# A Mamba block with expert weights: both ends of the schedule reordered, two decays of each group made five units ahead

## The chip, the cores and the metric

The kernel runs on one core of a Trainium2 chip. The metric is the device time of one execution in microseconds (us). Before the change it is 1063.78 us, the median of three runs (1063.17 to 1065.88).

## The reference, cut to what matters

For 32 sequences of 128 tokens and 128 channels, all in float32: rotate pairs of channels, normalise, run a selective scan forwards and backwards (16 states for each of 256 inner channels), mix both, gate, add the input; then an expert layer whose weights are picked by the sequence, and a feed-forward net of five layers.

```python
def _mamba(x, ...):
    xz = x @ in_proj_w.T;  xi, z = (xz[..., :DI], xz[..., DI:])
    xi = silu(causal_conv(xi, conv_w) + conv_b)
    dt, Bm, Cm = split(xi @ x_proj_w.T)
    delta = softplus(dt @ dt_proj_w.T + dt_proj_b);  A = -exp(A_log)
    # for each state n: h = exp(delta*A[n])*h + delta*xi*Bm[n];  y += h*Cm[n]
    y = (selective_scan(xi, delta, A, Bm, Cm) + xi * D) * silu(z)
    return y @ out_proj_w.T
y = gelu(concat(_mamba(xn), flip(_mamba(flip(xn)))) @ dim_reduce_w.T + b)
g = y @ glu_w.T + glu_b;  y = g[..., :H] * sigmoid(g[..., H:]) + skip
h = relu(x @ wi_e.T) @ wo_e.T                      # weights of expert e
h = silu(h @ w1.T * s1) * (h @ w2.T * s2)
h = gelu(h @ h1.T * s);  h = gelu(h @ h2.T * s);  out = x + h @ w3.T * s
```

## The kernel before

The sequences go through in nine groups: one of 2 sequences (256 columns), seven of 4 (512 columns), and one of 2 again. A group has 32 units: 16 states forwards (d = 0), 16 backwards (d = 1). Unit u passes through the engines in this order:

- GpSimd writes the drive of the unit, `du * b_row`, to one of 8 state rooms in SBUF (`drive`, L555), up to three units ahead.
- ScalarE writes the decay `exp(a_n * delta)` to one of two PSUM rooms `bank_d[u % 2]` in two instructions (`decays`, L702), two units ahead (`DECAY_LEAD`); before it the room must be free, so it waits for the product of unit u-2.
- VectorE scans (`scan`): for most units in place in the PSUM room (L905), then it multiplies by the row of C into the state room (L910). For the seven units of `POOL_UNITS` (3, 8, 12, 17, 21, 26, 30) the scan writes to the state room (L903), and GpSimd multiplies by the row of C (`weigh`, L560).
- TensorE adds the products up by transposes in PSUM (`sum_states`, L1190). After 16 units ScalarE copies the sum, and TensorE turns it back and adds `u * D` by a matmul with a diagonal matrix (`turn_y`, L1199 and L1201); VectorE multiplies by the gate (`gate_y`, L921).
- The rows of B and C come by DMA from DRAM, broadcast to all partitions, each kind into a ring of six rows.

All other layers are "fills": one PSUM bank filled by TensorE and taken by ScalarE or VectorE. Two banks (`bank_m`) serve all fills in turn. The order is written out by hand: every engine walks the same timeline in steps of half a unit, and the tables `FILL`, `TAKE_LAG`, `ACT_AT`, `VEC`, `GPS` and `LOADS` say at which time, counted in units from the start of its group, an engine issues each piece; `FIRST_GROUP`, `NEXT_TO_LAST` and `LAST_GROUP` shift it for groups 0, 7 and 8. The later layers of a group therefore run during the scans of the next two groups: the second Gelu layer of group g (`h2_`, taken by L751, Gelu at L758) is issued at 63 to 71, that is in the units 31 to 39 behind its own start of scans, while group g+1 ends and group g+2 begins. The tables set only the order on each engine; the times follow from semaphores.

ScalarE's functions come in table sets. Decays need the exponential set, the silu and the gelu another each, and each change is an `ACT_TABLE_LOAD` (L586).

For the ends: in group 0 both directions' inputs, the gates z and both halves are filled before the first scan; `step_sizes` (L535) and `inputs` (L544) on GpSimd make `delta` and `du` for both directions. In group 7 the h2 fills stand at 34 to 35 of group 8, ahead of the last `turn_y` at 36. The sigmoid of every group is made from exponential, logarithm and exponential (L719, L726, L728).

## Time and profile before

| what | value |
|---|---|
| median of three runs | 1063.78 us |
| the profiled execution: its own time | 1062.9 us |
| the profiled execution: span | 1060.6 us |
| mean granted TensorE clock | 0.96 of full speed |
| busy: TensorE, VectorE, ScalarE, GpSimd | 89%, 86%, 73%, 78% |
| chain that ended last | TensorE 46%, VectorE 19%, ScalarE 17%, issue 15%, GpSimd 3% |
| first scan, end of the last product of VectorE | 34.65 us, 1001.55 us |
| table loads of ScalarE | 69, 88.5 us |

The span runs from the first to the last instruction; the execution's own time is 2.3 us longer. The busy shares are means over three different stretches: a head without scans, the scans, and a tail in which only the late layers of groups 7 and 8 are left. The chain runs over all engines in turn, so a single share says little.

### The profile page before, as it was taken

Reading aid. Unit: us, or ns where it says so; the run is one execution under the profiler, and the core shown is the slowest. Engines: PE = TensorE matmul, PEld = TensorE weight load, DVE = VectorE, ACT = ScalarE, POOL = GpSimd, SP = SyncE. Lnnn points to the kernel's source line nnn. Section 1 sums busy time; section 2 is a strip of 40 time slices with the busy share of each in tenths; the row PEclk is TensorE's granted clock in tenths of the full one; section 3 lists DMA queues with packets and bytes.
Section 4 is the critical chain, followed back from the end, with each engine's and each line's share of the span. In section 5 each row is a group of like instructions: output and inputs, shape, how many; then the busy total and the mean of one; then the engine's idle time right before and its main releaser. Section 6 shows DMA issues by size and latency. Waiting matters only on the chain.

```text
span 1060.6 us, 13662 instructions
## 1 busy us (share of the span) xinstructions
PE 943.8 (89%) x4312; PEld 599.0 (56%) x4312; DVE 908.4 (86%) x718; ACT 778.1 (73%) x1233; POOL 829.5 (78%) x430
## 2 busy tenths in 40 slices
PE   5698678778999899999999999999999988998987
PEld 3455455656655467445755566545755575556455
DVE  1788999999999989999999999998999999968600
ACT  4757667778698768877688868877788758777532
POOL 0767998989988897989878997979878998866300
PEclk9697699898999999999999999999999999999999
DMA  3766675463646555654556554745555465536000
GB/s 95 253 204 208 187 216 180 137 218 116 195 142 194 171 165 147 208 167 144 160 163 183 168 167 123 237 147 168 153 164 187 151 178 146 165 121 169 0 11 6
DMA packets 97670, 167.43 MB, mean 158 GB/s; under 512 B 9920, under 2 KB 33408, under 8 KB 97344
## 3 DMA queue, kind: packets, MB, share of 16 engines
q1 hardware_dynamic: 97600, 166.57, 50.8%
q8 instruction: 35, 0.57, 0.2%
q14 instruction: 35, 0.29, 0.1%
HBM read 159.19 MB, written 7.34 MB: 157 GB/s over the span
## 4 chain that ended last, share of the span: by engine, by line
PE 46%; DVE 19%; ACT 17%; issue 15%; POOL 3%; DMA 0%; DVEq 0%; SPq 0%; POOLq 0%; ACTq 0%
DVE bank_d L905 12%; PE bank_m L1102 9%; PE bank_m L1026 9%; PE bank_y L1190 8%; ACT L586 5%; ACT bank_d L702 5%; PE bank_m L1109 5%; PE bank_m L1116 2%; DVE state L903 2%; PE bank_m L1075 2%; PE bank_m L1084 2%; DVE state L910 2%; POOL state L555 2%; PE bank_m L1044 1%; PE bank_m L1059 1%
## 5 line engine op out<-in xcount | busy, mean ns | idle before, releaser
L555 POOL TENSOR_TENSOR state<-du,b_rows 128x1024 f32<-128x1024 f32 (+1 forms) x288 | 603.9, 2121 | 92.6 <-PE bank_y L1190 91.7
L905 DVE TENSOR_TENSOR_SCAN bank_d<-bank_d,state 128x1024 f32<-128x1024 f32 (+1 forms) x225 | 461.2, 2050 | 44.0 <-ACT bank_d L702 38.6
L702 ACT ACTIVATE bank_d<-delta,a_neg 128x512 f32<-128x512 f32 (+1 forms) x576 | 345.0, 634 | 104.5 <-DVE state L910 94.2
L1190 PEld LDWEIGHTS bank_y<-ident,state 128*128 128x128 f32 x2048 | 240.4, 145 | 81.7 <-issue 55.5
L1190 PE MATMUL bank_y<-ident,state 128*128 128x128 f32 x2048 | 263.3, 281 | 17.8 <-POOL state L560 11.7
L910 DVE TENSOR_TENSOR state<-bank_d,c_rows 128x1024 f32<-128x1024 f32 (+1 forms) x225 | 248.8, 1106 | 7.8
L560 POOL TENSOR_TENSOR state<-state,c_rows 128x1024 f32<-128x1024 f32 (+1 forms) x63 | 134.2, 2131 | 16.4 <-DVE state L903 16.4
L903 DVE TENSOR_TENSOR_SCAN state<-bank_d,state 128x1024 f32<-128x1024 f32 (+1 forms) x63 | 128.7, 2042 | 1.2 <-ACT bank_d L702 1.2
L1109 PE MATMUL bank_m<-hidA,h_s 128*128 128x512 f32 (+1 forms) x256 | 111.8, 584 | 15.6 <-ACT relu_dt L683 9.7
L1026 PE MATMUL bank_m<-xnT,w_conv 128*128 128x508 f32 (+7 forms) x288 | 115.3, 550 | 4.8 <-DVE x1T L930 3.1
L1102 PE MATMUL bank_m<-hidB,h_s 128*128 128x512 f32 (+1 forms) x256 | 110.3, 584 | 1.7 <-DVE hidB L944 0.8
L586 ACT ACT_TABLE_LOAD x69 | 88.5, 1283 | 1.9 <-PEq L1266 0.7
L1109 PEld LDWEIGHTS bank_m<-hidA,h_s 128*128 128x128 f32 x256 | 48.3, 197 | 69.3 <-issue 50.7
L1026 PEld LDWEIGHTS bank_m<-xnT,w_conv 128*128 128x128 f32 x288 | 54.1, 195 | 51.0 <-issue 43.1
L1102 PEld LDWEIGHTS bank_m<-hidB,h_s 128*128 128x128 f32 x256 | 48.5, 194 | 56.0 <-issue 52.3
L535 POOL TENSOR_TENSOR delta<-relu_dt,log_dt 128x1024 f32<-128x1024 f32 (+1 forms) x18 | 38.2, 2122 | 24.5 <-ACT log_dt L693 24.5
L1044 PE MATMUL bank_m<-dbc,w_dt_s 64*128 64x512 f32 (+1 forms) x72 | 37.5, 612 | 15.0 <-ACT dbc L677 12.6
L751 ACT ACTIVATE hidB<-bank_m,col 128x512 f32<-128x512 f32 (+1 forms) x32 | 21.1, 661 | 34.6 <-PE bank_m L1109 34.0
L921 DVE TENSOR_TENSOR gated<-bank_y,z 128x1024 f32<-128x1024 f32 (+1 forms) x18 | 19.8, 1102 | 26.5 <-PE bank_y L1201 26.5
L520 POOL TENSOR_TENSOR rstd<-var_eps,half_power 128x4 f32<-128x4 f32 (+1 forms) x9 | 8.6, 951 | 35.1 <-issue 20.1
L1075 PE MATMUL bank_m<-x1T,wsel 128*128 128x128 f32 x240 | 31.7, 278 | 3.9 <-DVE x1T L934 3.5
L1075 PEld LDWEIGHTS bank_m<-x1T,wsel 128*128 128x128 f32 x240 | 29.6, 191 | 7.7 <-DVE x1T L930 3.9
(143 smaller groups left out, 1011.8 us busy)
## 6 DMA issues: line engine op xcount, KB each, us to landing
b_rows<-bc_store SPq DMA_DIRECT2D x256, 256.0 KB, 4.2
c_rows<-bc_store SPq DMA_DIRECT2D x256, 256.0 KB, 4.3
wsel<-merged SPq DMA_DIRECT2D x32, 512.0 KB, 3.5
merged<-hidA SPq DMA_DIRECT2D x8, 512.0 KB, 3.1
h_s<-in_h SPq DMA_DIRECT2D x2, 1024.0 KB, 8.9
xin<-in_x SPq DMA_DIRECT2D x7, 256.0 KB, 3.9
out<-cT SPq DMA_DIRECT2D x7, 256.0 KB, 3.1
wsel<-in_factors SPq DMA_DIRECT2D x8, 160.0 KB, 3.7
```

What stands on the lines that cost most here:

```text
L555: nc.gpsimd.tensor_tensor(split(unit_state(u)), du[:, d, :, :width(g)], per_half(b_rows, u), ALU.mult).then_inc(S.bx_ready, 1)
L560: nc.gpsimd.tensor_tensor(split(unit_state(u)), split(unit_state(u)), per_half(c_rows, u), ALU.mult).then_inc(S.weighed, 1)
L586: act.preload_act_table_set(name)
L702: ins = act.activation(split(unit_decay(u))[:, h], delta[:, d, h, :width(g)], ACT.Exp, scale=a_neg[:, h, n:n + 1])
L903: dve.tensor_tensor_scan(drive, decay, drive, 0.0, ALU.mult, ALU.add).then_inc(S.unit_done, 1)
L905: dve.tensor_tensor_scan(decay, decay, drive, 0.0, ALU.mult, ALU.add).then_inc(S.scanned, 1)
L910: dve.tensor_tensor(split(unit_state(u)), split(unit_decay(u)), per_half(c_rows, u), ALU.mult).then_inc(S.unit_done, 1)
L1026: ins = pe.matmul(dst, w, src, start=(m == 0), stop=(m == TAPS - 1))
L1075: ins = pe.matmul(bank(g, f"hid{f}")[:, at], wsel[:, s, f * P:(f + 1) * P], x1T[:, at], start=True, stop=True)
L1102: ins = pe.matmul(bank(g, f"h1_{f}"), h1_s[:, q, f * P:(f + 1) * P], hidB[:, q, :width(g)], start=(q == 0), stop=(q == FC - 1))
L1109: ins = pe.matmul(bank(g, f"h2_{f}"), h2_s[:, q, f * P:(f + 1) * P], hidA[:, q, :width(g)], start=(q == 0), stop=(q == FC - 1))
L1190: ins = pe.matmul(bank_y[:, h, s * P:(s + 1) * P], split(unit_state(u))[:, h, s * LEN:(s + 1) * LEN], ident[:, :], start=(n == 0 and s == ...
```

## The change

- `early`, a room in SBUF of 1024 columns: the decays of units 8 and 17 of every group (`AHEAD`) are made there five units ahead instead of two. The other units share the two PSUM rooms in turn, so the first units behind 8 and 17 wait for one unit earlier than before. The ring of C rows falls from six to four to make room.
- `u * D` of groups 7 and 8 goes through ScalarE (`skip`): a scaled copy into `gated`, added up by transposes with the states; the matmul with the diagonal goes.
- Group 0: VectorE makes `delta` and `du` of d = 0 (`first_inputs`); `ur` and `z` are filled behind the inputs of d = 0, `ur` gets its Silu in a second step (`front` at 4.0). The conv weights are made behind `rotate`.
- Group 7's second Gelu layer is taken with Gelu from the bank; its fills h2_0 to h2_3, w3 and tok move to 75, 68, 78.5, 81.5, 82.5 and 88, that is into the chain of group 8's late layers (h2_1 at 36.0 of group 8, behind the turn, then out at 36.5, glu1 37.5, glu0 39, h2_0 43, res 44, hid 44.5 to 46, h2_2 46.5, wo 48, h2_3 49.5).
- Group 8's sigmoid is half of tanh plus a half, with the gelu's table set.
- Slots move by half a unit or so in the inner groups, by more in groups 0, 1 (a new table `SECOND_GROUP`), 7 and 8. In the inner groups `out` is issued at 37.5 instead of 38.0 and the second Gelu at 70.5 instead of 71.0.

```diff
-ROWS = 6
+ROWS, C_ROWS = 6, 4
+AHEAD, AHEAD_LEAD = (8, 17), 5
-DIRECT = {"gate": NG - 1, "h1_": NG - 1, "h2_": NG - 1}
+BY_SCALAR = NG - 2
+DIRECT = {"gate": NG - 1, "h1_": NG - 1, "h2_": NG - 2}
...
+        early = sb("early", [P, HALVES * GT])
...
+        def ahead(u):
+            return u % UNITS in AHEAD
+        in_psum = [u for u in range(TOTAL) if not ahead(u)]
+        psum_at = {u: i for i, u in enumerate(in_psum)}
+        in_early = [u for u in range(TOTAL) if ahead(u)]
...
         def unit_decay(u):
-            return bank_d[u % 2][:, :HALVES * width(u // UNITS)]
+            room = early if ahead(u) else bank_d[psum_at[u] % 2]
+            return room[:, :HALVES * width(u // UNITS)]
...
                 use_table(EXP_LN)
-                if n == 0:
+                if n == 0 or ahead(u):
                     act.wait_ge(S.starts_marked, 2 * g + d + 1)
-                wait(act, S.unit_done, u - 1)
+                before = [v for v in in_early if v < u][-1:] if ahead(u) else in_psum[:psum_at[u]][-2:-1]
+                if before:
+                    act.wait_ge(S.unit_done, before[0] + 1)
...
+            def skip(g, d):
+                wait_u(act, g, d)
+                if g > 0:
+                    wait_filled(act, g - 1, "out")
+                w = width(g)
+                for h in range(HALVES):
+                    ins = act.activation(gated[:, d, h, :w], (u_f, u_r)[d][:, g % 2, h, :w], ACT.Copy, scale=c("skip_d", h))
+                ins.then_inc(S.skipped, 1)
...
+            def first_inputs():
+                w = width(0)
+                dve.wait_ge(S.log_ready, 1)
+                dve.tensor_tensor(delta[:, 0, :, :w], relu_dt[:, :, :w], log_dt[:, :, :w], ALU.add).then_inc(S.delta_ready, 1)
+                dve.wait_ge(S.delta_ready, 1)
+                wait_u(dve, 0, 0)
+                dve.tensor_tensor(du[:, 0, :, :w], delta[:, 0, :, :w], u_f[:, 0, :, :w], ALU.mult).then_inc(S.du_ready, 1)
...
+                if n == NST - 1 and g >= BY_SCALAR:
+                    pe.wait_ge(S.skipped, 2 * (g - BY_SCALAR) + d + 1)
+                    for h in range(HALVES):
+                        for s in range(sequences(g)):
+                            pe.matmul(bank_y[:, h, s * P:(s + 1) * P], gated[:, d, h, s * LEN:(s + 1) * LEN], ident[:, :],
+                                      start=False, stop=False, is_transpose=True, skip_group_check=True)
...
+            dve.wait_ge(S.exp_done, made_as[u] + 1)
```

## Rows read from the trace of the kernel before

**Rows 1.** The page's first part: busy time and share of each engine.
```profile
PE 943.8 (89%) x4312; PEld 599.0 (56%) x4312; DVE 908.4 (86%) x718; ACT 778.1 (73%) x1233; POOL 829.5 (78%) x430
```

**Rows 2.** Busy time by stretch (us, PE, PEld, DVE, ACT, POOL, PEclk, DMA, GB/s).
```profile
0.00:34.60 34.60, 18.16 (x64) 13.30 (x64) 6.01 (x25) 18.45 (x44) 6.11 (x14) 0.97 0.40 120
...
262.00:379.00 117.00, 108.90 (x504) 66.06 (x503) 111.69 (x78) 94.62 (x141) 103.35 (x48) 1.00 0.55 173
...
1001.60:1018.20 16.60, 15.93 (x44) 7.63 (x44) 0.00 (x0) 4.90 (x7) 0.00 (x0) 1.00 0.00 0
1018.20:1061.00 42.80, 33.25 (x149) 24.36 (x148) 4.57 (x9) 15.59 (x27) 0.00 (x0) 0.99 0.04 10
```

**Rows 3.** Groups of VectorE's instructions by shape: GpSimd-weighed units, full width.
```profile
L903 DVE TENSOR_TENSOR_SCAN state<-bank_d,state 128x1024 f32<-128x1024 f32 x49 | 111.7, 2279 | 0.6 <-ACT bank_d L702 0.6
```

**Rows 4.** Waits of VectorE, 262 to 846 us (total, times, longest).
```profile
DVE bank_d L905 <- ACT bank_d L702: 21.8, 12, 2.2
DVE x1T L930 <- PE bank_m L1059: 3.5, 4, 0.9
DVE gated L921 <- PE bank_y L1201: 3.2, 6, 0.6
```

**Rows 5.** VectorE's timeline: scans of units 8 and 9, group 5.
```profile
605.19 2.28 DVE L903 TENSOR_TENSOR_SCAN state<-bank_d,state 128x1024 f32<-128x1024 f32 x1
609.59 2.30 DVE L905 TENSOR_TENSOR_SCAN bank_d<-bank_d,state 128x1024 f32<-128x1024 f32 x1 [2.13 <-ACT bank_d L702]
```

**Rows 6.** The timeline of ScalarE between the decays of units 8 and 9.
```profile
601.84 1.30 ACT L702 ACTIVATE bank_d<-delta,a_neg 128x512 f32<-128x512 f32 x2 [0.44 <-DVE state L910]
...
603.16 1.28 ACT L586 ACT_TABLE_LOAD   x1
...
604.46 1.91 ACT L758 ACTIVATE hidB<-hidB 128x2048 f32<-128x2048 f32 x1
...
608.26 1.30 ACT L702 ACTIVATE bank_d<-delta,a_neg 128x512 f32<-128x512 f32 x2
```

**Rows 7.** VectorE instructions with both inputs in SBUF, and GpSimd beside them (timeline).
```profile
114.20 1.40 DVE L883 TENSOR_TENSOR xc<-xc,scaled 128x512 f32<-128x512 f32 x1
...
343.38 0.68 DVE L883 TENSOR_TENSOR xc<-xc,scaled 128x512 f32<-128x512 f32 x1
...
110.40 4.66 POOL L555 TENSOR_TENSOR state<-du,b_rows 128x1024 f32<-128x1024 f32 x2
115.01 1.72 POOL L560 TENSOR_TENSOR state<-state,c_rows 128x512 f32<-128x512 f32 x1
```

**Rows 8.** GpSimd beside the scans of units 8 and 17, group 5 (timeline).
```profile
602.73 7.00 POOL L555 TENSOR_TENSOR state<-du,b_rows 128x1024 f32<-128x1024 f32 x3
...
640.99 2.36 POOL L555 TENSOR_TENSOR state<-du,b_rows 128x1024 f32<-128x1024 f32 x1 [1.91 <-PE bank_y L1190]
...
639.24 2.28 DVE L903 TENSOR_TENSOR_SCAN state<-bank_d,state 128x1024 f32<-128x1024 f32 x1
```

**Rows 9.** The page's DMA issues: KB each, median us from issue to landing.
```profile
c_rows<-bc_store SPq DMA_DIRECT2D x256, 256.0 KB, 4.3
```

**Rows 10.** The timeline of the head, to the first scan.
```profile
13.17 2.05 PE L1032 MATMUL bank_m<-xnT,w_z_s 128*128 128x256 f32 x4 [0.75 <-ACT xnT L634]
...
15.01 9.04 PE L1026 MATMUL bank_m<-xnT,w_conv 128*128 128x256 f32 x32
...
30.52 1.26 POOL L535 TENSOR_TENSOR delta<-relu_dt,log_dt 128x512 f32<-128x512 f32 x1 [19.63 <-ACT log_dt L693]
...
34.65 1.23 DVE L905 TENSOR_TENSOR_SCAN bank_d<-bank_d,state 128x512 f32<-128x512 f32 x1 [4.64 <-POOL state L555]
```

**Rows 11.** Waits of VectorE, 925 to 1001.6 us.
```profile
DVE bank_d L905 <- ACT bank_d L702: 10.7, 6, 4.0
```

**Rows 12.** TensorE's timeline behind the last scan.
```profile
1002.93 13.97 PE L1109 MATMUL bank_m<-hidA,h_s 128*128 128x512 f32 x32 [0.67 <-ACT hidA L758]
...
1016.74 0.59 PE L1199 MATMUL bank_y<-u_r,skip 128*128 128x256 f32 x2
```

More of the change, by code:

```diff
@@ L133, in slot @@
     at = table[name] if k is None else table[name][k]
-    shifts = {0: FIRST_GROUP, NG - 2: NEXT_TO_LAST, NG - 1: LAST_GROUP}.get(g, {})
-    return at + shifts.get(name, 0.0)
+    shifts = {0: FIRST_GROUP, 1: SECOND_GROUP, NG - 2: NEXT_TO_LAST, NG - 1: LAST_GROUP}.get(g, {})
+    return at + shifts.get(name, 0.0) + (0.0 if k is None else shifts.get(f"{name}:{k}", 0.0))
 def first_pair(g):
@@ L280, in wait_u @@
         def wait_u(eng, g, d):
-            if g == 0:
-                wait_taken(eng, g, *(("uf0", "uf1"), ("ur0", "ur1"))[d])
+            if g + d == 0:
+                wait_taken(eng, g, "uf0", "uf1")
             else:
-                eng.wait_ge(S.u_ready, 2 * (g - 1) + d + 1)
+                eng.wait_ge(S.u_ready, 2 * g + d)
         def wait_hidden(eng, g, name):
@@ L531, in step_sizes @@
             def step_sizes(g, d):
+                if g + d == 0:
+                    return
                 wait(pool, S.log_ready, 2 * g + d + 1)
-                wait(pool, S.exp_done, UNITS * (g - 1) + NST * d + NST)
+                if g > 0:
+                    pool.wait_ge(S.exp_done, max(made_as[UNITS * (g - 1) + NST * d + n] for n in range(NST)) + 1)
                 w = width(g)
@@ L764, in table_of @@
             def table_of(g, name):
-                if g == 0 and name[0] == "u":
+                if g == 0 and name[:2] == "uf":
                     return SILU
                 if name == "glu1":
-                    return EXP_LN
+                    return EXP_LN if g < NG - 1 else GELU
                 if name == "out" or name[:3] in ("h1_", "h2_") and direct(g, name[:3]):
@@ L822, in _ @@
                     for d in range(2):
+                        if g >= BY_SCALAR and rel == slot(ACT_AT, g, "skip", d):
+                            skip(g, d)
                         if rel == slot(ACT_AT, g, "softplus", d):
@@ L827, in _ @@
                 for g, rel in groups[::-1]:
-                    if rel == slot(ACT_AT, g, "silu", 0):
+                    if rel == slot(ACT_AT, g, "front"):
                         silu_front(g)
-                    if not direct(g, "gate") and rel == slot(ACT_AT, g, "silu", 1):
+                    if not direct(g, "gate") and rel == slot(ACT_AT, g, "silu"):
                         silu_gate(g)
                 for g, rel in groups[::-1]:
-                    if rel == slot(ACT_AT, g, "silu", 0):
+                    if rel == slot(ACT_AT, g, "front"):
                         silu_z(g)
                 u = unit_at(at, DECAY_LEAD)
-                if u is not None:
+                if u is not None and not ahead(u):
+                    decays(u)
+                u = unit_at(at, AHEAD_LEAD)
+                if u is not None and ahead(u):
                     decays(u)
@@ L969, in _ @@
             rotation_tables()
-            conv_weights()
-            skip_weights()
             for at, groups in timeline():
+                if at == slot(GPS, 0, "delta", 0):
+                    first_inputs()
                 u = unit_at(at, 0)
```

95 lines of the change are left out of this document (53 added, 42 removed), and 47 rows, old and new, of tables (FILL, FIRST_GROUP, LAST_GROUP, NEXT_TO_LAST).

## The prediction
> **What bounds the kernel now.** The page's busy shares [rows 1] name TensorE, but the busy time by stretch splits the span into three parts with different limits [rows 2]. In the head (34.6 us) no engine is busy for more than 18.5 us: it is a chain of dependent steps up to the first scan. From 34.6 to 1001.6 us VectorE is the bound: in an inner group it is busy 111.7 of 117 us, TensorE 108.9, GpSimd 103.4, ScalarE 94.6. In the tail TensorE is the bound: 15.93 + 33.25 = 49.2 us busy of 59.4. So a gain can come from a shorter chain ahead of the first scan, from VectorE's waits in between, or from TensorE's work and gaps behind the last scan; and the inner groups can give little, since TensorE would be the bound at 109.
>
> Then the waits of VectorE over the five inner periods, 262 to 846 us [rows 4]: 21.8 us in 12 waits for ScalarE's decays, 3.5 and 3.2 us for two TensorE results. That is 5.7 us per group. The timeline says which decays are late: five of the twelve stand ahead of unit 9 and take 2.12 us each [rows 5], the rest stand ahead of unit 0 (1.6 to 2.2 us) and unit 27. ScalarE's own timeline shows why unit 9 is late [rows 6]: the decay of unit 8 waits for the product of unit 6 (begins at 601.84), then come the table load, the Gelu of 2048 columns, another take and another table load, and the decay of unit 9 begins only at 608.26.
>
> **Decays made ahead: the gain.** With unit 8's decay made at unit 3, the table load can follow unit 7's decay. From 603.16 it moves up by the 1.30 us of unit 8's decay and the wait of 0.44 ahead of it, 1.7 us; `out` is issued one unit earlier, so the take behind the Gelu should not hold this up. Unit 9's decay would then end near 607.9 and its scan could begin at 608.0 instead of 609.6: about 1.5 of the 2.12 us. The waits ahead of units 0 and 27 come from the first Gelu at 29.5, whose place in the order is as before; I leave them. Unit 17 has no wait of this kind in any inner group, so its early decay gains nothing there. Bound from below: all waits ahead of unit 9 gone, 1.0 (group 2) + 5 x 2.12 + 4.0 (group 8, the longest of [rows 11]) = 15.6 us.
>
> **Decays made ahead: the cost.** The early room is in SBUF, and the drive is in SBUF too, so the scans of units 8 and 17 read two SBUF operands; before, every scan read its decay from PSUM. The only VectorE instruction of the inner loop with both inputs in SBUF is L883 [rows 7]. Where GpSimd is idle it takes 0.68 us. At 114.20 it took 1.40 us: GpSimd's instruction ran until 115.06, and VectorE ended 0.54 us after that; GpSimd's next instruction, 1.26 us long elsewhere, took 1.72 us and began its real work when VectorE was through. The two shut each other out for whole instructions. So an early scan waits for what is left of GpSimd's instruction (0 to 2.3 us), and then holds GpSimd up for its own 2.28 us [rows 3].
>
> What is left can be read at the same places of this trace. For unit 8 of group 5, GpSimd is in the second of three drives of 2.33 us each, which ends 2.2 us behind the scan's start; for unit 17 GpSimd waits for TensorE and nothing is left [rows 8]. Read in the same way in all nine groups: unit 8: 0.7, 0.8, 1.2, 2.1, 2.1, 2.2, 2.1, 0, 0.9; unit 17: 0.75, 1.5, 0, 0, 0, 0, 0, 2.1, 0.5. Now the sum. In groups 3 to 6 a scan 8 that starts 2.1 us late ends at 609.6, exactly when scan 9 began before: gain and cost cancel, 0. Group 2: +0.2. Groups 0 and 1, where nothing waited at unit 9: +1.5. Group 7: nothing left, -1.5. Group 8: 4.0 of wait, 0.9 of cost, and part of the ScalarE chain stays: -2.5. Unit 17 in all: +4.9. Together +2.6 us. The bounds: -15.6 us (no exclusion and every wait gone), and with the full 2.3 us at 14 full-width scans and 1.25 us at four narrow ones, 37 us, less the 10 us of waits they fall on, +27 us. I take +2.6, which rests on the phases of this very trace, though the phases will move.
>
> The Trainium skill has this rule in "SBUF — State Buffer", section "Who interferes with whom": a VectorE instruction with two SBUF inputs contends with a GpSimd instruction that reads SBUF, and whichever is first holds the shared pair until its instruction ends. By that rule the cost stands as summed here; without it group 2 would give 1.0, the inner groups 5 x 1.5 and group 8 about 3 us, which makes the total 14 us lower. The row at 114.20 agrees with the rule.
>
> GpSimd loses up to 2 x 2.28 us per group. It is busy 103.4 of 117, and its drives are waiting for TensorE to free state rooms, so 4.6 of 13.6 us of slack go. Near unit 9 the drives are two units ahead (about 7 us): no new wait of VectorE.
>
> **Four rows of C.** The load for unit u now waits for the product of u-4 instead of u-6; the queue of SP holds the loads of B behind it. A load lands in 4.3 us at the median [rows 9], three units last over 10 us, and for a unit weighed by GpSimd still two units are left: 0, at most 2 us per group if GpSimd falls behind.
>
> **The head.** Removed ahead of the first scan: the z fills (2.05 us) and half of the 9.04 us of conv fills, 4.5 us [rows 10]; `rotate` starts 0.9 us earlier, since it no longer stands behind the conv weights; `delta` and `du` on VectorE take 0.68 us each by [rows 7] instead of 1.26 us each [rows 10], -1.2 us. That is -8.6 us for the drive. But on ScalarE the takes of ur0, ur1, z0 and z1 stand ahead of the first decay, and on VectorE two merges of expert weights stand ahead of the first scan, the second ready only near 29.1 us. So I get the first scan at 29.8 instead of 34.65: -4.85 us, and one merge (0.65) that used to interrupt the scans is already done: -5.5 us. Group 0 itself pays: two more table loads (2 x 1.28 [rows 6]) and a Silu at slot 4.0, of which two units of lead hide most, and GpSimd's delta of d = 1 has to wait for a softplus later in ScalarE's order: +1 (-3 to +5).
>
> **The end of the scans.** VectorE waits 10.7 us for decays in group 8 [rows 11]; one of the six is counted above. Group 8's slots are mostly new; the diagonal matmuls go (0.59 us a piece at this width [rows 12], double that in group 7) and the transposes that replace them cost about half. ScalarE has eight more copies. I take -2.5 us (-7 to +4).
>
> **The tail.** The last turn waits for 13.97 us of h2 fills of group 7 [rows 12]. That is no gain of 14 us: the fills are only moved behind it, and TensorE's 49.2 us must all be done. What can go is the 10.2 us of gaps: the last 2.7 are the final copy and store, the three between the deep layers of group 8 (0.6 each) have no filler, and the ones around out, hid, wo and gate, near 3 us, get h2 fills. Two diagonal matmuls (1.2 us) go, 0.4 us of transposes come. -2.5 - 0.8 = -3.3 us (-1 to -7). The tanh form saves two table loads that lay beside 3.6 us of TensorE work: 0.
>
> **The sum.** +2.6 - 5.5 + 1 - 2.5 - 3.3 = -7.7 us against the profiled execution: a span of 1052.9 and an own time of 1055.2 us. Its 1062.9 stands 0.9 us below the median, so on the runs' scale I say 1056.
>
> **Rivals.**
> (A) The exclusion hardly hurts: early scans start just ahead of GpSimd's instructions instead of just behind (it is 0.13 to 0.26 us in groups 3 to 6), and then GpSimd waits, not VectorE. Ahead-decays give -8 instead of +2.6, less the 10.3 us of the ends, total -18: 1045. For it: small phase shifts decide it. Against: GpSimd is busy 88% in these groups.
> (B) The exclusion decides: each early scan waits 1.5 us or more and GpSimd's lost 4.6 us per group make its products late, so that TensorE, busy 93% and in order, sums late and everything behind slips. Place: units 8 to 12 and 17 to 20 of each full group. 14 x 2 us = +28 - 10 = +18, less 10.3 at the ends: +8, 1071. It decides from a mean wait of about 1.4 us per early scan. Against: unit 17 finds GpSimd idle in five groups.
> (C) The ends are worth nothing: group 0 gives back what the head gained (d = 1 late), and the reordered group 8 waits elsewhere. Then only +2.6 - 3.3: 1063, no change.
>
> **Chances.** Forecast 0.45, A 0.20, B 0.18, C 0.17. My forecast's own range is 1050 to 1062. 0.3%, about 3.2 us, is what a measurement here can tell from no change. Faster: most of the forecast (0.43), all of A, a little of C: 0.65. Same: 0.14. Slower: B and a part of C: 0.21. The range, 1043 to 1070, takes in A and nearly all of B.
>
> **What would show it.** First scan near 30 us. Scans that read `early` longer than 2.28 us, up to 4.6, beside a running GpSimd instruction, and GpSimd's instructions beside them up to 2.3 us longer; period of an inner group 116 to 117. The last gate within 5 us of the last product, with h2 fills between the layers of group 8, and 55 to 57 us from the last product to the end. I am wrong if early scans all take 2.28 us, if the period leaves 115 to 118, or if the scans of group 0 begin earlier and end no earlier.

## The result, and the profile after

The changed kernel takes 1060.55 us (median of six runs, 1059.2 to 1064.38) against 1063.47 for the kernel before in the same job (1062.82 to 1065.88): a ratio of 0.9969, 95% interval 0.9958 to 0.998. It is faster by 2.9 us where 7.7 were forecast. The stated range held the time; the sum behind it did not stand. The profiled execution has a span of 1057.0 us, 3.6 less than before.

The page's first part, after (as [rows 1]):

```profile
PE 944.2 (89%) x4320; PEld 603.2 (57%) x4320; DVE 920.4 (87%) x722; ACT 779.4 (74%) x1241; POOL 855.6 (81%) x428
```

VectorE and GpSimd are busy 12.0 and 26.1 us longer, though each does about the same work. This is how it looks when one engine is shut out while its instruction already counts as running. The groups of VectorE's scans say where (columns as in [rows 3]):

```profile
L978 DVE TENSOR_TENSOR_SCAN state<-bank_d,state 128x1024 f32<-128x1024 f32 x35 | 79.8, 2280 | 1.5 <-ACT bank_d L745 1.5
L978 DVE TENSOR_TENSOR_SCAN state<-early,state 128x1024 f32<-128x1024 f32 x14 | 41.3, 2953 | 0.0
```

The same line takes 2280 ns with the decay in PSUM and 2953 ns with the decay in SBUF. At full width that is 14 x 0.67 = 9.4 us; the four narrow ones (256 columns) add 2.0.

An inner period by stretch (columns as [rows 2]): TensorE and ScalarE do no more than before, VectorE 1.5 and GpSimd 4.0 us more.

```profile
262.00:379.00 117.00, 108.69 (x504) 65.97 (x504) 113.14 (x78) 92.52 (x138) 107.30 (x48) 1.00 0.56 167
```

The waits of VectorE over the same five periods as [rows 4], in this kernel 254 to 836.5 us:

```profile
DVE bank_d L980 <- ACT bank_d L745: 13.2, 9, 1.9
DVE gated L996 <- PE bank_y L1286: 5.0, 5, 2.3
DVE x1T L1026 <- PE bank_m L1194: 2.3, 1, 2.3
```

The wait for decays fell from 21.8 to 13.2 us: the 2.12 us ahead of unit 9 are gone in all these groups but group 6, where 0.88 is left. In group 5, the place of [rows 5], [rows 6] and [rows 8], the timelines of VectorE, ScalarE and GpSimd now read:

```profile
596.94 2.54 DVE L978 TENSOR_TENSOR_SCAN state<-early,state 128x1024 f32<-128x1024 f32 x1
599.40 2.27 DVE L980 TENSOR_TENSOR_SCAN bank_d<-bank_d,state 128x1024 f32<-128x1024 f32 x1
...
592.21 1.28 ACT L626 ACT_TABLE_LOAD   x1
593.50 1.92 ACT L817 ACTIVATE hidB<-hidB 128x2048 f32<-128x2048 f32 x1
595.33 0.66 ACT L765 ACTIVATE gy<-bank_m,col 128x512 f32<-128x512 f32 x1
...
592.63 9.00 POOL L595 TENSOR_TENSOR state<-du,b_rows 128x1024 f32<-128x1024 f32 x3
```

The early scan lost only 0.25 us: it began 4.31 us into GpSimd's three drives, just before the second ended. The three drives took 9.00 us instead of 7.00, so here GpSimd paid. The forecast had the scan just behind the start of the second drive and 2.2 us late.

The starts of the first scans of the groups give the periods (us, group 0 to 7): before 76.1, 112.6, 116.5, 116.8, 118.5, 117.1, 118.5, 114.0; after 76.6, 112.5, 117.3, 114.1, 115.6, 116.4, 124.0, 115.8. The first scan begins at 31.06 (before 34.65), the last at 998.7 (999.6). So 3.6 us are gained in the head and 6.3 in groups 3 to 5; 1.2 are lost in groups 0 to 2, 5.5 in group 6, 1.8 in group 7 and 0.5 in group 8's scans. In group 6 TensorE waits 3.06 us for `gy` and VectorE 2.29 for w3, and the scan of unit 17 is 1.93 us late. The tail follows, TensorE's timeline behind the last product (which ends at 1000.64; [rows 12] are before's):

```profile
1002.97 3.60 PE L1187 MATMUL bank_m<-hidA,h_s 128*128 128x512 f32 x8
1006.40 1.89 PE L1129 MATMUL bank_m<-gated,w_fused 128*128 128x256 f32 x8
1008.95 1.10 PE L1137 MATMUL bank_m<-xnT,w_glu_s 128*128 128x256 f32 x4 [0.66 <-ACT xnT L765]
1010.18 3.70 PE L1187 MATMUL bank_m<-hidA,h_s 128*128 128x512 f32 x8
...
1043.53 7.14 PE L1187 MATMUL bank_m<-relu_dt,h_s 128*128 128x256 f32 x32 [0.61 <-issue]
```

The h2 fills of group 7 stand between the layers of group 8, and 56.4 us pass from the last product to the end, where it was 59.05.

### The profile page after: what moved, and what is told of

The parts are those of the page before. It is cut to its first block, busy times and chain, and to the rows that moved or that the text cites. A ratio compares the mean times of both kernels' runs of the same rounds, so it can differ in the third digit from the quotient of the medians.

```text
span 1057.0 us, 13719 instructions
## 1 busy us (share of the span) xinstructions
PE 944.2 (89%) x4320; PEld 603.2 (57%) x4320; DVE 920.4 (87%) x722; ACT 779.4 (74%) x1241; POOL 855.6 (81%) x428
## 4 chain that ended last, share of the span: by engine, by line
PE 44%; ACT 17%; issue 16%; DVE 14%; POOL 8%; DMA 1%; SPq 0%; DVEq 0%; POOLq 0%; ACTq 0%
DVE bank_d L980 9%; PE bank_y L1274 9%; PE bank_m L1104 8%; PE bank_m L1180 7%; POOL state L595 5%; PE bank_m L1187 5%; ACT bank_d L745 4%; ACT L626 4%; PE bank_m L1153 3%; DVE state L978 2%; POOL state L600 2%; PE bank_m L1194 2%; PE bank_m L1162 2%; PE bank_m L1169 2%; PE bank_m L1122 1%
## 5 line engine op out<-in xcount | busy, mean ns | idle before, releaser
L595 POOL TENSOR_TENSOR state<-du,b_rows 128x1024 f32<-128x1024 f32 (+1 forms) x288 | 629.1, 2210 | 53.6 <-PE bank_y L1274 46.1
L980 DVE TENSOR_TENSOR_SCAN bank_d<-bank_d,state 128x1024 f32<-128x1024 f32 (+1 forms) x225 | 461.2, 2050 | 32.0 <-ACT bank_d L745 30.9
L745 ACT ACTIVATE bank_d<-delta,a_neg 128x512 f32<-128x512 f32 (+1 forms) x540 | 322.6, 634 | 78.2 <-DVE state L985 73.5
L1274 PEld LDWEIGHTS bank_y<-ident,state 128*128 128x128 f32 x2048 | 243.9, 147 | 92.5 <-issue 63.4
L1274 PE MATMUL bank_y<-ident,state 128*128 128x128 f32 x2048 | 270.2, 284 | 25.9 <-DVE gated L996 12.5
L600 POOL TENSOR_TENSOR state<-state,c_rows 128x1024 f32<-128x1024 f32 (+1 forms) x63 | 134.1, 2128 | 16.7 <-DVE state L978 15.7
L1104 PE MATMUL bank_m<-xnT,w_conv 128*128 128x508 f32 (+7 forms) x288 | 118.4, 557 | 4.5 <-DVE x1T L1005 2.4
L1187 PE MATMUL bank_m<-hidA,h_s 128*128 128x512 f32 (+1 forms) x256 | 112.5, 585 | 5.7 <-ACT hidA L817 4.6
L1180 PE MATMUL bank_m<-hidB,h_s 128*128 128x512 f32 (+1 forms) x256 | 107.8, 573 | 0.8 <-DVE hidB L1019 0.8
L978 DVE TENSOR_TENSOR_SCAN state<-bank_d,state 128x1024 f32<-128x1024 f32 (+1 forms) x45 | 92.0, 2044 | 3.4 <-ACT bank_d L745 3.4
L576 POOL TENSOR_TENSOR delta<-relu_dt,log_dt 128x1024 f32<-128x1024 f32 (+1 forms) x17 | 38.9, 2287 | 13.1 <-ACT log_dt L733 13.1
L978 DVE TENSOR_TENSOR_SCAN state<-early,state 128x1024 f32<-128x1024 f32 (+1 forms) x18 | 48.2, 2678 | 0.0
L1169 PE MATMUL bank_m<-cT,w_s 128*128 128x512 f32 (+1 forms) x64 | 32.1, 625 | 10.1 <-ACT hidA L801 9.6
```

The source lines that it names most:

```text
L595: nc.gpsimd.tensor_tensor(split(unit_state(u)), du[:, d, :, :width(g)], per_half(b_rows, u), ALU.mult).then_inc(S.bx_ready, 1)
L600: nc.gpsimd.tensor_tensor(split(unit_state(u)), split(unit_state(u)), per_half(c_rows, u), ALU.mult).then_inc(S.weighed, 1)
L745: ins = act.activation(split(unit_decay(u))[:, h], delta[:, d, h, :width(g)], ACT.Exp, scale=a_neg[:, h, n:n + 1])
L978: dve.tensor_tensor_scan(drive, decay, drive, 0.0, ALU.mult, ALU.add).then_inc(S.unit_done, 1)
L980: dve.tensor_tensor_scan(decay, decay, drive, 0.0, ALU.mult, ALU.add).then_inc(S.scanned, 1)
L1104: ins = pe.matmul(dst, w, src, start=(m == 0), stop=(m == TAPS - 1))
```

## The experiments

All were timed against the kernel before in the same job and on the same chip, each 4 to 12 times (before's medians there: 1064.2 to 1065.1). "Ends" is everything in the change but the early decays and the C ring, so it includes the half-unit moves of the inner groups. Differences below are differences of ratios times 1064 us.

| kernel | median, us | ratio to before, 95% |
|---|---|---|
| E1 ends, no early decay, C ring 4 | 1077.99 | 1.0117 [1.0101, 1.0133] |
| E2 before + early 8 and 17, C ring 4 | 1078.89 | 1.0138 [1.0116, 1.0159] |
| E3 before, 8 and 17 in SBUF but two ahead, C ring 4 | 1078.14 | 1.0118 [1.0095, 1.0141] |
| E4 after, early 8 alone | 1054.51 | 0.9896 [0.9882, 0.9911] |
| E5 before + C ring 4 | 1068.04 | 1.0030 [1.0018, 1.0042] |
| E6 ends, no early decay, C ring 6 | 1076.24 | 1.0103 [1.0084, 1.0122] |
| E7 E4 with rings of 5 and 5 | 1054.94 | 0.9908 [0.9883, 0.9934] |
| E8 after, early 8 and 30 | 1059.82 | 0.9961 [0.9945, 0.9977] |
| E9 E6 with before's slots in groups 2 to 6 | 1075.09 | 1.0107 [1.0091, 1.0123] |
| E10 before + early 8 alone, C ring 4 | 1066.85 | 1.0013 [1.0000, 1.0026] |
| E11 E4 with before's slots in groups 2 to 6 | 1064.31 | 1.0000 [0.9987, 1.0013] |
| E12 E4 with group 7's late fills ahead of the turn | 1061.76 | 0.9967 [0.9955, 0.9980] |
| E13 ends, 8 in SBUF but two ahead | 1074.39 | 1.0080 [1.0058, 1.0103] |
| E14 after, early 17 alone | 1081.03 | 1.0154 [1.0129, 1.0180] |
| E15 E4 with the decay three units ahead | 1058.54 | 0.9939 [0.9917, 0.9961] |
| E16 E4 with the conv weights ahead of `rotate` | 1055.21 | 0.9909 [0.9883, 0.9934] |

### The change taken apart

E1 is the new kernel with no unit made early, E2 the old one with the early decays added, E3 the old one with nothing but the room changed:

```diff
# E1
-AHEAD, AHEAD_LEAD = (8, 17), 5
+AHEAD, AHEAD_LEAD = (), 5
# E3, in before (with C_ROWS = 4)
-            return bank_d[u % 2][:, :HALVES * width(u // UNITS)]
+            room = early if u % UNITS in (8, 17) else bank_d[u % 2]
+            return room[:, :HALVES * width(u // UNITS)]
```

> The changed kernel without decays made ahead: all decays in the two PSUM rooms, two units ahead; the reordered ends and the four rows of C stay. Theory 1 (the exclusion of VectorE and GpSimd takes back what the early decays gain): this kernel is as fast as the changed one, 1060.5 us, within 2 us, and the period of groups 3 to 5 is back at 116.8 us, but no scan takes over 2.31 us. Theory 2 (the early decays gain 8 us or more and the reordered ends cost it): this kernel is slower than the changed one by 5 us or more, at 1065 or above. The first scan stays at 31.1 us by both.

> The kernel before, with only the decays of units 8 and 17 made five units ahead in SBUF and four rows of C; every slot, head and tail as before. Theory 1: about 1063 us (within 2 us of before): waits ahead of unit 9 fall by 1.5 to 2 us in groups 2 to 8, scans of units 8 and 17 take up to 4.6 us. Theory 2: 1056 us or less. First scan at 34.65 us by both.

> The kernel before, the decays of units 8 and 17 written to the SBUF room, but two units ahead and with the waits of before: the price of the exclusion without any gain; four rows of C. By the phases read in the trace of before (16.8 us of remains, of which 4 x 2.1 us at unit 8 fall ahead of a wait for the decay of unit 9, which they do not shorten): +13 to +17 us, 1077 to 1080, if the wait for unit 9 follows the scan of unit 8; if the decay of unit 9 is ready meanwhile (it does not wait for unit 8), the late scan 8 uses up that wait, and only +5 to +8 us stay, 1069 to 1071. If there is no exclusion: 1063.5, no change. Scans of 8 and 17 between 2.28 and 4.6 us, and GpSimd's instructions beside them up to 4.6 us.

E1 is 1.17% slower than before, not 10 us faster, so the ends alone cost, and the early decays give back 1.48% (15.7 us) on top of them. E2 shows the opposite in the old slots; at 1078.9 us it is 16 us above the slower of its two expectations. The exclusion is real: in E3 nothing moved but the room (and the C ring), and scan 8 of groups 3 to 6 takes 4.22 to 4.34 us. E3's time fell in the first of its branches, its trace in the second: the late scan used up the wait ahead of unit 9 (0.1 to 0.2 us left). All 18 early scans together are 23.5 us longer than their PSUM form in E3, 21.6 in E2 and 11.4 in the changed kernel. In E2 scan 8 is as long as in E3, and GpSimd's timeline beside it shows the phase:

```profile
607.67 8.99 POOL L567 TENSOR_TENSOR state<-du,b_rows 128x1024 f32<-128x1024 f32 x3
```

```profile
610.21 4.31 DVE L920 TENSOR_TENSOR_SCAN state<-early,state 128x1024 f32<-128x1024 f32 x1
```

This scan begins 2.54 us into the three drives, just behind the start of the second, and waits 2.03 us for it: the 2.1 us of the forecast. In the changed kernel it began 4.31 us into them and lost 0.25. GpSimd's three drives take 9.0 us in both.

The wait is not bounded by one instruction of the other engine. In group 1 of E3 and of E10 (below; unit 8 alone, old slots) scan 8 took 7.60 and 7.64 us. E10's VectorE and GpSimd there:

```profile
140.87 7.64 DVE L920 TENSOR_TENSOR_SCAN state<-early,state 128x1024 f32<-128x1024 f32 x1
...
137.05 7.00 POOL L567 TENSOR_TENSOR state<-du,b_rows 128x1024 f32<-128x1024 f32 x3
144.03 2.34 POOL L556 TENSOR_TENSOR du<-delta,u_r 128x1024 f32<-128x1024 f32 x1
```

The scan stood through the rest of the second drive, the third, and `du`, though both of the latter began behind it. In E2 a scan with the same start (140.87) took 3.00 us. No run shows what decides between the two.

### Unit 8 alone, and the ring of C rows

E4 has `AHEAD = (8,)`, E5 is the kernel before with `C_ROWS = 4`, and E6 is E1 with `C_ROWS = 6`.

> The changed kernel with only unit 8's decay made ahead; unit 17's goes back to PSUM, two units ahead. Unit 17 gained nothing at its place and cost scans of 4.49, 4.21, 4.00 and 2.82 us instead of 2.28 in groups 2, 6, 7 and 1, 6.4 us. Theory 1: faster than the changed kernel by 3 to 6 us, 1055 to 1058. Rival (the waits behind unit 17 are TensorE's and come anyway, as the turn of group 6 at 765.6): within 1.5 us of the changed kernel.

> The kernel before with four rows of C instead of six and nothing else. Theory 1 (the short ring is what made the last four kernels slow: the load of C for unit u stands in SP's queue until GpSimd has weighed unit u-4, and the loads of B behind it come late): slower than before by 8 to 14 us, 1072 to 1078, and SP's waits for the weighing of L560 rise from 119 us to about 200 in 262 to 846 us. Theory 2 (the ring costs nothing, the exclusion costs 14 us in the one kernel and the reordered ends 14 us in the other): within 2 us of before.

> The changed kernel without early decays and with six rows of C: the reordered ends alone. Theory 1: the ends bring what their places show, 3.6 us ahead of the first scan and 2.7 behind the last product, so 1056 to 1059, and the kernel with four rows (1078) was slow by its ring. Theory 2: still at 1074 or more.

E4 has the lowest median of all: 1.04% below before and 0.73% (7.8 us) below the change as made, a little more than expected. Unit 17 early only costs. E5 puts the smaller ring at +3.2 us, between its expectations. The queue of SP waits longer, 262 to 846 us, before and then E5: the load of a C row (L449, L450) now waits for the product made from the row four loads back, GpSimd's above all.

```profile
SPq L449 <- POOL state L560: 118.8, 25, 7.1
```

```profile
SPq L450 <- POOL state L561: 186.9, 27, 11.0
SPq L450 <- DVE state L911: 134.3, 64, 5.6
```

But the periods of groups 2 to 5 are before's within 0.2 us, so that is not where it costs. Groups 0, 1 and 6 are longer, by 1.6, 1.3 and 3.4 us. In group 6 what comes late is not a C row but the next x, whose load stands behind those of C in the same queue. It is issued 103.9 us into the group, just behind a C row's, instead of 98.5; ScalarE stands 4.04 us for it, and the decay of unit 29 behind it is late for VectorE:

```profile
798.92 0.32 SPq L450 DMA_DIRECT2D c_rows<-bc_store  x1
799.34 0.37 SPq L395 DMA_DIRECT2D xin<-in_x  x1
...
803.99 0.40 ACT L615 ACTIVATE scaled<-xin,rot 128x128 f32<-128x128 f32 x1 [4.04 <-DMA xin<-in_x]
...
806.49 2.30 DVE L906 TENSOR_TENSOR_SCAN bank_d<-bank_d,state 128x1024 f32<-128x1024 f32 x1 [3.92 <-ACT bank_d L703]
```

With the ends the ring's share (E1 against E6) is 0.14%, within the intervals. So E6, the ends with nothing else, costs about 11 us. Its profiled execution is 16.0 us longer than before's: head and group 0 gain 5.2, group 8 and the tail 1.8, and groups 1 to 6 lose 3.0, 5.8, 5.2, 1.9, 2.3 and 4.7.

### Where one early decay gains 23 us

E1 against E4 is one decay per group: 2.21%, 23.5 us (22.2 in the two profiled executions). The waits ahead of unit 9 account for a part: 2.1 to 2.3 us in each of groups 3 to 7, 16.9 us in all nine groups of E1 and 3.7 in E4. TensorE's timeline in group 3, E1:

```profile
377.66 1.63 PE L1137 MATMUL bank_m<-gy,w_glu_s 128*128 128x512 f32 x2 [4.06 <-ACT gy L765]
...
379.93 2.68 PE L1274 MATMUL bank_y<-ident,state 128*128 128x128 f32 x16
382.45 3.60 PE L1194 MATMUL bank_m<-hidB,w_s 128*128 128x512 f32 x8
```

and VectorE's in E1:

```profile
380.16 2.30 DVE L980 TENSOR_TENSOR_SCAN bank_d<-bank_d,state 128x1024 f32<-128x1024 f32 x1 [2.12 <-ACT bank_d L745]
...
386.09 0.75 DVE L1026 SCALAR_TENSOR_TENSOR x1T<-bank_m,col,x1T 128x512 f32<-128x512 f32 x1 [2.37 <-PE bank_m L1194]
```

The same place in E4, TensorE:

```profile
367.81 1.10 PE L1137 MATMUL bank_m<-gy,w_glu_s 128*128 128x512 f32 x2 [1.36 <-ACT gy L765]
...
369.19 1.91 PE L1274 MATMUL bank_y<-ident,state 128*128 128x128 f32 x16
```

Three things hang on that one decay here. VectorE waits 2.12 us ahead of unit 9. TensorE, in order, stands 4.06 us for `gy`, which ScalarE makes behind the Gelu. And TensorE's clock falls; the stretches of E1 (columns as in [rows 2]) are the one with the wait, the one behind it, and the next:

```profile
372.50:377.60 5.10, 1.09 (x9) 0.80 (x7) 5.07 (x3) 5.05 (x6) 5.10 (x3) 1.00 0.77 258
377.60:382.40 4.80, 4.74 (x22) 3.85 (x23) 2.68 (x2) 4.79 (x7) 4.74 (x4) 0.64 0.42 84
382.40:386.00 3.60, 3.60 (x11) 1.69 (x10) 1.28 (x2) 1.49 (x3) 3.60 (x3) 1.00 0.00 0
```

Behind 4.06 us of standing the granted clock reads 0.64, a mixture of the two levels, 1.2 and 2.4 GHz, and 16 transposes take 2.68 us instead of 1.91. Then w3's fill is late, and VectorE waits for it another 2.37 us. In E4 the wait is 1.36 us, the clock stays at 1.00, and w3 is in time. In the kernel before the wait was 2.34 us, the clock stayed at 1.00, and w3 was in time too.

The other groups agree on the clock and less on w3. In groups 3 to 7 of E1 the waits for `gy` are 3.66 to 4.25 us, and the lower level is granted behind each. In before it is granted behind none of the four of 2.23 to 2.34 us, but behind the 2.12 us of group 7 (0.66 from 841 to 846 us), so the length of one wait doesn't settle it alone. VectorE's wait for w3 shows only in groups 2, 3 and 6 of E1 (2.78, 2.37, 2.30 us) and in group 6 of E4 (2.30). Over the whole execution E4's VectorE waits 14.7 us less for decays (ahead of L980, 37.5 instead of 52.2 us), 5.1 less for w3 and about 6 less in smaller waits, and its early scans take 4.4 us back: 21 of the 22.2 us. Over 262 to 846 us TensorE's waits for `gy` in before, E1 and E4:

```profile
PE bank_m L1059 <- ACT gy L712: 11.4, 5, 2.3
```

```profile
PE bank_m L1137 <- ACT gy L765: 16.4, 4, 4.2
```

```profile
PE bank_m L1137 <- ACT gy L765: 7.3, 5, 3.1
```

E1 has four waits in this window, since its fifth (3.66 us) falls behind it. So the new slots had made a hidden wait long enough to come to the surface, and the early decay of unit 8 took it away again. Three runs ask which property of it does so. E10 is the kernel before with only unit 8 early; E13 keeps E1's order but puts unit 8's decay in SBUF; E15 makes it three units ahead (`AHEAD_LEAD = 3`).

```diff
# E13, in E1
-            room = early if ahead(u) else bank_d[psum_at[u] % 2]
+            room = early if u % UNITS == 8 else bank_d[u % 2]
```

> The kernel before with only unit 8's decay made ahead, and four rows of C; all slots of before. With units 8 and 17 ahead it took 1079. Scans 17 there cost 7.8 us more than 2.28 each, so -8: 1069 to 1072, if the cost is the scan's own lengthening; theory 2, GpSimd's lost time at unit 17 carries over to unit 8 of the next group (scan 8 took 4.25 us there, 2.52 in the changed kernel): below 1065.

> The kernel after the change, where the decay of unit 8 alone still goes to the SBUF room but is made two units ahead, at its old place in ScalarE's order; unit 17 is in PSUM. Theory (what helps is the place in ScalarE's order, ahead of the table load for Gelu): nothing of the 23.5 us between no early decay (1078.0) and unit 8 alone (1054.5) comes back, and the wait of scan 8 for GpSimd is added, 7 groups x 1 to 2 us: 1078 to 1090, with w3's take still waiting 2 us and more per group. Rival (the relief comes from unit 8 leaving the two PSUM rooms, or from the phase that a longer scan 8 gives to what follows): 1065 or less.

> Unit 8 alone ahead, but three units ahead instead of five: its decay is issued one unit earlier than before the change. Theory (it must only stand ahead of the table change; how far ahead does not matter): the Gelu chain still loses one decay, so 1054.5 as with five units, 1052 to 1057. Rival (distance matters: three ahead it stands just behind unit 7's decay wait, for a product that is late, and the table load moves up by less): between 1060 and 1070, with a wait of TensorE for gy near 3 us.

In the old slots it is worth 1.8 us (E10 against E5, whose intervals overlap): the wait ahead of unit 9 goes, and scan 8 takes 4.24 to 4.29 us in groups 3 to 6 instead of 2.28. In E13 the wait for `gy` is back, 4.10 us in group 4, and so is most of the time: 19.6 of the 23.5 us come with making the decay early. That moves it in ScalarE's order and also leaves a PSUM room free sooner for the decays behind it, which E13's rule does not. The trace of E4 says that the order does it: in groups 3 to 6 the decay of unit 9 begins 0.28 to 1.98 us behind the product of unit 7, which would have freed its room under the old rule too, with no wait of ScalarE in front of it. The room alone (E13 against E1) gave 3.9 us where I had expected nothing or a loss; the two intervals touch, the runs are of different jobs, and why stays open. Three units ahead is 4.6 us slower than five, between the two expectations: TensorE's waits for `gy` grow from 1.36 to about 1.87 us in groups 3 to 5 and from 3.06 to 4.29 in group 6. Its profiled span isn't longer (1055.7 against 1056.9), but E4's profiled execution (1059.1) is the slowest of its five, 4.6 us above their median, so E4's trace shows less than its runs gained.

### Other units

> The changed kernel with the decays of units 8 and 30 made ahead instead of 8 and 17. With unit 30's made early, unit 31's waits for unit 28 instead of 29, so the table load and the first Gelu at 29.5 come up to 3.4 us sooner and the wait of 1.6 to 2.2 us ahead of unit 0 of each group goes. Theory 1 (a long ScalarE piece between two decays is what makes VectorE wait, and one free room ahead of it cures that): -1 to -2 us per full group against the kernel with unit 8 alone (1054.5), 1044 to 1049, if scan 30 meets little of GpSimd's work. Rival (the exclusion at unit 30 takes it back, as GpSimd is in a row of drives there): 1053 to 1060.

> The kernel after the change with only unit 17 made five ahead; unit 8 back in PSUM two ahead. Theory (the gain is unit 8's alone, since only its decay stands in front of the table loads of Gelu and gy; unit 17 costs 6 us as it did between unit 8 alone and both): no early decay 1078.0 plus 0 to 6: 1078 to 1084. Rival (ScalarE is late all over in the reordered schedule, any decay out of its way helps, and 17 would relieve the takes around units 12 to 17): 1066 to 1072.

E8 makes unit 30 early beside unit 8. VectorE's waits for decays over 262 to 846 us, E4 and E8:

```profile
DVE bank_d L980 <- ACT bank_d L745: 19.4, 15, 3.5
```

```profile
DVE bank_d L980 <- ACT bank_d L745: 12.5, 13, 3.5
```

The waits fell by 6.9 us and the kernel became 6.9 us slower (its profiled span, 1056.3, is E4's within 0.6): less waiting for one engine is not less time. The scans of unit 30 say where a part went: they now take 2.95 to 4.13 us in groups 2 to 7 instead of 2.28, 8.5 us more in all nine groups. E14 completes the square of the two units: neither 1.0117, 8 alone 0.9896, 17 alone 1.0154, both 0.9969. Unit 17 costs 3.9 us by itself and 7.8 beside unit 8. Its scans take 4.49, 4.21 and 4.00 us in groups 2, 6 and 7 of the changed kernel; VectorE and GpSimd in group 6:

```profile
748.74 4.21 DVE L978 TENSOR_TENSOR_SCAN state<-early,state 128x1024 f32<-128x1024 f32 x1
...
746.13 8.98 POOL L595 TENSOR_TENSOR state<-du,b_rows 128x1024 f32<-128x1024 f32 x3 [2.80 <-PE bank_y L1274]
```

The scan begins 2.61 us into three drives, again just behind the start of the second. It is late by 1.93 us. No run splits the 7.8 us further.

### The slots

E9 and E11 give groups 2 to 6 the slots of the kernel before, without an early decay and with unit 8's; E12 puts `h2_0`, `h2_2`, `h2_3`, `w3` and `tok` of group 7 back ahead of the last turn (and `h2_1` one unit earlier); E7 shares the rows evenly.

```diff
# E12, in E4 (the entries that change, cut out of their lines)
-"h2_2": 13.5, "h2_3": 13.5, "w3": 10.0, "h2_0": 9.0, "tok": 14.0, "h2_1": 4.5
+"h2_2": 1.5, "h2_3": -1.0, "w3": -0.5, "h2_0": 0.0, "tok": 0.0, "h2_1": 3.5
```

> The reordered ends without early decays and with six rows of C (1076 with the new inner slots), but groups 2 to 6 at the slots of the kernel before. Theory 1 (the half-unit moves of the inner groups only pay with unit 8's decay early; without it TensorE waits 4.1 us for gy instead of 2.3, and VectorE 2.4 us for w3): the inner periods return to 116.8 to 118.5, 1060 to 1064. Theory 2 (the reordered groups 0, 1, 7 and 8 are what cost): 1072 or more.

> The changed kernel with unit 8 ahead (1054.5), groups 2 to 6 at the slots of before. Theory 1 (slots and early decay pay only together): 1062 or more, with scans 8 near 4.2 us. Rival (the inner slots are worth nothing, the early decay all): 1053 to 1056.

> The changed kernel with unit 8 ahead (1054.5), but group 7's h2, w3 and tok fills back at the slots of before, ahead of the last turn. By the sum (TensorE's work behind the last product is the same, only its gaps are filled): +2 to +4, 1056.5 to 1058.5. Rival: the fills ahead of the turn hold the whole of group 8's chain, +8 or more.

> The changed kernel with only unit 8 made ahead, and the same SBUF shared out as five rows of B and five of C instead of six and four. Theory 1 (the C ring's wait for the weighing is the cost): 1050 to 1053, against 1054.5 with six and four. Rival (B is as tight as C, since GpSimd drives three units ahead): 1057 or more.

E9 equals E6 in time, so the old inner slots alone don't give the 11 us back. In the profiles they do help where they stand, groups 2 to 6 being 9.8 us shorter than in E6, but group 7 behind them is 5.6 us longer and group 1 0.7. E11 against E4 is 11.1 us: with the early decay the new inner slots are what lets it gain. Part of that is the phase: scan 8 of groups 4 to 6 takes 4.24 to 4.32 us in E11 and 2.52 to 2.53 in E4, 5.3 us in all, which is the whole difference of the two profiled spans (5.0); the rest shows in the medians alone. E12 against E4 is 7.6 us: in the profiles the scans end 5.8 us earlier without the reorder (the last product at 994.8 against 1000.6 in E4 and after alike), and the tail is 62.3 us long instead of 56.4. That made the two profiled executions equal, and the runs put the reorder well ahead, by more than the 2 to 4 us expected. E7 is E4 within its interval, between its two expectations: the ring is not what limits E4.

### The head

`rotate` did start earlier, at 7.02 instead of 7.83 us, and yet the normalised input was ready no sooner. GpSimd's first power instruction in the changed kernel:

```profile
8.68 1.54 POOL L558 TENSOR_TENSOR rstd<-var_eps,half_power 128x2 f32<-128x2 f32 x1 [7.15 <-DVE var_eps L971]
```

Before, it took 0.71. VectorE's product of the conv weights, two SBUF inputs, ran beside it (8.43 to 9.65 us). E16 puts those weights back ahead of `rotate`:

```diff
             rotation_tables()
+            conv_weights()
+            skip_weights()
...
                         rotate(g)
-                        if g == 0:
-                            conv_weights()
-                            skip_weights()
```

> Unit 8 alone ahead, with the conv and skip weights made ahead of rotate on VectorE again, as in the kernel before the change. Theory (GpSimd's first power instruction took 1.54 us instead of 0.71 only because VectorE's weight instructions, both inputs in SBUF, ran beside it, which ate the 0.8 us that the earlier rotate had gained): rotate starts near 7.8 us, the power instruction takes 0.7 us again, xnT is ready at the same time as with unit 8 alone, the first scan starts within 0.3 us of its 31 us, and the time is 1054.5 within 2. Rival (the reorder does help the head): the first scan 0.8 us later or more.

```profile
10.09 0.71 POOL L558 TENSOR_TENSOR rstd<-var_eps,half_power 128x2 f32<-128x2 f32 x1 [8.56 <-DVE var_eps L971]
```

The power instruction takes 0.71 us again, the first scan begins at 30.59 (E4: 31.35), and the time is E4's. Moving these weights bought nothing. Nor is the earlier scan due to it: `rotate` now starts at 8.44 us, and the normalised input is ready 0.45 us later than in E4.

What moves the first scan between kernels of the same head is TensorE's clock. In the changed kernel the trace's first clock record, at full level, begins at 18.77 us. The conv matmuls start 0.42 us apart ahead of it and 0.21 us apart behind it, as they would at 1.2 and 2.4 GHz. (The view of stretches prints a clock of 1.00 for the time without a record.) In E1 the first record begins at 16.27 us, with the same step in the matmuls:

```profile
13.27 5.14 PE L1104 MATMUL bank_m<-xnT,w_conv 128*128 128x256 f32 x16 [0.66 <-ACT xnT L674]
...
29.91 1.22 DVE L980 TENSOR_TENSOR_SCAN bank_d<-bank_d,state 128x512 f32<-128x512 f32 x1
```

So E1's first scan is 1.15 us ahead of the changed kernel's, where its expectation had 31.1 for both. Over all traces with the reordered head the first record begins between 16.27 and 19.35 us and the first scan between 29.91 and 31.43. At like moments the reorder of the head is worth 3.3 us: 33.42 (E3, record at 16.65) against 30.12 (E9, 16.71), and 34.65 (before, 19.14) against 31.35 (E4, 19.23).

## Why the prediction was wrong, step by step

- **What bounds the kernel.** Right as far as it went: VectorE is the bound from the first scan to the last. What it left out is TensorE's wait for `gy`, 11.4 us over [rows 4]'s five periods, made by the very ScalarE chain of [rows 6]: it did not reach VectorE then.
- **Decays made ahead, +2.6 us.** This step failed. Measured, they are worth -15.7 us in the new slots (after against E1) and +11.5 in the old ones (E2 against E5). The gain at unit 9 came (no wait left in groups 3 to 5, 1.94 us off at that place in group 5). The exclusion is there too, 11.4 us over the 18 scans. But the phases were taken from the old trace, and they moved: 0.25 us in groups 3 to 6 where 2.1 to 2.2 were read. And the early decay also shortens TensorE's chain behind the Gelu (its wait for `gy` is 4.06 us without it and 1.36 with it), which the sum did not contain at all. "I take +2.6, which rests on the phases of this very trace, though the phases will move" names the first weakness and then ignores it. The rule of the Trainium skill ("SBUF — State Buffer", section "Who interferes with whom") was confirmed by E3 as far as the two instructions exclude each other; its cost hangs on where in GpSimd's instruction the scan begins, and was mostly between 0.25 and 2.1 us. That whichever is first goes first does not hold throughout: the scan of 7.64 us in E10 was passed by two GpSimd instructions that began behind it.
- **Unit 17, +4.9.** Near enough: +7.8 beside unit 8, +3.9 alone. Nearly full waits, 1.7 to 2.2 us, appeared in groups 2, 6 and 7, where the old phases had shown one, in group 7. The scans alone are 7.0 us longer.
- **Four rows of C, 0.** Mis-sized: +3.2 us in the old slots. The 4.3 us landing time was read right and groups 2 to 5 lose nothing, but the price comes by another load of the same queue: the x row in group 6, for which ScalarE stands 4.04 us. The forecast had named only the loads of B behind those of C. It was within the 2 us a group that was allowed for.
- **The head, -5.5.** Mis-sized: -3.6 for the first scan, where 4.85 of the 5.5 were forecast. The first scan stands at 31.06, not 29.8. The drive starts 4.2 us earlier (29.07 against 33.28), not 8.6. The 0.9 us of `rotate` were lost to the exclusion, by the very rule used elsewhere in the sum. The fills gave 4.4 us instead of 6.55: the first 16 matmuls of group 0's conv take 6.47 us and 16 more ten microseconds later 3.68, because TensorE runs slowly until its first clock record at 18.77 us whatever it fills, so removing the z fills gave their slow time to the conv. Then TensorE stands 0.61 us for a Silu that the reverse conv used to cover, and GpSimd's residual (0.72) now stands ahead of the drive. The scan itself begins behind the second merge, which started at 30.45 instead of 29.1. E1's first scan at 29.91, with the same head, would have looked like a hit: that is the luck of an early clock record, and at like moments the reorder is worth 3.3 us.

```profile
13.10 6.47 PE L1104 MATMUL bank_m<-xnT,w_conv 128*128 128x256 f32 x16 [0.66 <-ACT xnT L674]
...
23.41 3.68 PE L1104 MATMUL bank_m<-xnT,w_conv 128*128 128x256 f32 x16 [0.50 <-ACT relu_dt L723]
27.20 1.16 PE L1110 MATMUL bank_m<-xnT,w_z_s 128*128 128x256 f32 x4
```

- **Group 0 +1, end of the scans -2.5.** Group 0's period is 0.5 longer, near the +1. The scans of groups 7 and 8 take 2.3 longer where 2.5 less were forecast.
- **The tail, -3.3.** Right: -2.7 in the profiles.
- **The ends together, -10.3.** This is the other failed step. Each end looked at by itself gained (-3.6 and -2.7), yet E6 costs 11 us, in groups 1 to 6: the shifted slots put waits into the stretches in between, such as the 4.06 us for `gy`. The prediction summed the two ends as if the 900 us of scans between them ran as before, and put the slots moved in the inner groups at nothing without a reason. Against before, E9, whose groups 2 to 6 have their old slots, is 3.8 us longer in group 1, 2.8, 3.1, 2.1 and 3.7 in groups 2, 3, 5 and 6, 1.7 shorter in group 4 and 5.8 longer in group 7, so a group with its old slots seems to suffer from what its neighbours do. Which slot does it wasn't found; that stays open.
- **The sum.** -15.7 for the early decays and +12.4 for the ends with the smaller ring (E1) stand where +2.6 and -10.3 were forecast. Both main terms had the wrong sign, and their errors nearly cancelled. That the time came out faster and inside the range is luck and says little for the argument.
- **The rivals.** B's mechanism fits E2 and E3 (21.6 and 23.5 us of longer scans), A's (GpSimd waits instead) groups 3 to 6 of the changed kernel. C's premise, ends worth nothing, was too mild.

## What to carry to other kernels

When an instruction is moved out of one engine's way, follow what that engine makes next for every other engine: here one decay in front of a Gelu released VectorE by 2 us and TensorE by 2.7, and without it TensorE's wait, hidden before the change, came back in some groups as a second wait of VectorE. A price that hangs on how two engines' instructions are staggered is a range from nothing to a whole instruction and sometimes more (5.4 us in E10), and a schedule edit anywhere re-draws it; so measure each candidate alone (one unit early was worth 7.8 us more than two) before keeping the set. A load that waits holds up every load behind it in the same queue, so look at those too. And slots that suit one version of a kernel need not suit it with one part taken away: undo single parts to see which of them carries the others.

## What the runs showed that was not expected

- Standing can cost TensorE twice. Behind a wait of 4.06 us the granted clock read 0.64 over 4.8 us and the same 16 transposes took 2.68 instead of 1.91 us; behind waits of 2.34 (before, group 3) and 1.36 us it read 1.00 and they took 1.91. Before's group 7 is the exception: 2.12 us of waiting, then 2.87 us for the 16 transposes.
- A scan can be passed over more than once: 7.64 us instead of 2.28, with two GpSimd instructions that began behind it done first.
- The two engines' exclusion is not only a matter of long instructions: a two-element-wide power instruction on GpSimd took 1.54 us instead of 0.71 beside one VectorE product.
- A granted clock of 1.00 can mean that there is no record. From 13.1 to 16.0 us of the changed kernel the view reads 1.00 while the conv matmuls start 0.42 us apart, twice what they take later. The trace's clock records begin at 18.77 us, and there the spacing halves.
- Several variants scatter more than the kernel before: E7 from 1050.6 to 1058.8 us, before from 1063.07 to 1066.02 in its job. The profiled spans alone would have ranked E4 and E12 as equal. When TensorE's clock first rises (16.27 to 19.35 us) moves the first scan by 1.5 us and so makes up a part of it.
